# Cross-attention with image-prompt tokens: the store of a block's second query tile moves into the next round

## The reference

```python
q = _split_heads(hidden_states @ w_q, HEADS)
k = _split_heads(text @ w_k, HEADS)
v = _split_heads(text @ w_v, HEADS)
out_text = _merge_heads(_sdpa(q, k, v))
mask_ip = _ip_mask(bbox, B, S, hidden_states.dtype)
k_ip = _split_heads(ip_h @ w_k_ip, HEADS)
v_ip = _split_heads(ip_h @ w_v_ip, HEADS)
out_ip = _merge_heads(_sdpa(q, k_ip, v_ip, mask=mask_ip))
out = out_text + IP_SCALE * out_ip
out = out @ w_out + b_out
out = out + residual
```

## Time and profile before

| | |
|---|---|
| timed runs | 734.43, 734.0, 729.98 us (median 734.0) |
| profiled execution, device time | 729.49 us |
| its span, first to last instruction | 727.7 us |
| TensorE matmul busy | 688.1 us (95%) |
| VectorE busy | 540.1 us (74%) |
| ScalarE, POOL busy | 288.3 us (40%), 213.5 us (29%) |
| mean granted TensorE clock | 0.979 |

### The profile page before, as it was taken

One profiled execution on the slowest core, in us unless ns is written; L12 is line 12 of the kernel. 1 busy time (PEld: TensorE's weight loads), 2 busy tenths in 40 slices (PEclk: granted clock), 3 DMA queues, 4 the chain that ended last, 5 costly groups with the idle time before them and its releaser, 6 DMA issues.

```text
span 727.7 us, 18922 instructions
## 1 busy us (share of the span) xinstructions
PE 688.1 (95%) x6410; PEld 628.2 (86%) x6410; DVE 540.1 (74%) x1686; ACT 288.3 (40%) x626; POOL 213.5 (29%) x359
## 2 busy tenths in 40 slices
PE   4979778999999999999999999999999999999987
PEld 3567467989999998989999999999999989899876
DVE  5341539878787979797878788787879797978764
ACT  1031117153534435261617162535444261617061
POOL 7100004324150504142423324151505042423223
PEclk9879999999999999999999999999999999999979
DMA  9935954253434444433435263534344444434310
GB/s 266 323 98 137 267 147 121 66 155 92 136 90 134 102 127 103 140 89 102 130 89 156 68 163 82 147 96 127 98 127 103 133 96 125 104 92 114 90 49 37
DMA packets 79543, 89.52 MB, mean 123 GB/s; under 512 B 10680, under 2 KB 63416, under 8 KB 79492
## 3 DMA queue, kind: packets, MB, share of 16 engines
q1 hardware_dynamic: 79016, 88.45, 44.7%
q10 hardware_dynamic: 492, 0.61, 0.4%
HBM read 39.21 MB, written 10.62 MB: 68 GB/s over the span
## 4 chain that ended last, share of the span: by engine, by line
PE 75%; DMA 8%; DVE 7%; SPq 6%; issue 2%; ACT 1%; ACTq 0%; POOL 0%; DVEq 0%
PE psum L1019 32%; PE psum L1124 9%; PE psum L1076 7%; PE psum L1108 6%; PE psum L1103 5%; DMA q_stack<-aux_a 4%; SPq L457 3%; PE psum L1132 3%; PE psum L901 3%; PE psum L1133 2%; SPq L429 2%; DMA wo_raw<-in_L_xattn_w_v_ip 2%; PE psum L1147 2%; PE psum L980 2%; PE psum L1130 1%
## 5 line engine op out<-in xcount | busy, mean ns | idle before, releaser
L522 POOL TENSOR_TENSOR attn<-o_parts 128x128 f32<-128x128 f32 x160 | 73.8, 461 | 418.9 <-DVE o_parts L844 418.9
L803 DVE TENSOR_REDUCE neg_max<-psum 128x2 f32<-128x292 f32 x320 | 144.7, 452 | 64.0 <-PE psum L1076 63.4
L1019 PE MATMUL psum<-wo_both,at_hi 128*128 128x320 f32 x640 | 153.2, 313 | 0.0
L1019 PE MATMUL psum<-xt_hi,wq_hi 128*128 128x256 f32 x400 | 114.9, 287 | 1.4 <-DVE xt_lo L773 1.4
L1076 PE MATMUL psum<-k_stack,q_stack 104*128 104x154 f32 x640 | 112.6, 286 | 3.5 <-DVE neg_max L804 1.5
L1019 PE MATMUL psum<-xt_hi,wq_lo 128*128 128x256 f32 x400 | 112.1, 280 | 0.0
L1019 PE MATMUL psum<-xt_lo,wq_hi 128*128 128x256 f32 x400 | 112.0, 280 | 0.0
L831 DVE TENSOR_TENSOR p_lo<-psum,p_hi 128x512 f16<-128x512 f32 x160 | 107.9, 682 | 2.8 <-ACT psum L657 2.8
L1019 PEld LDWEIGHTS psum<-wo_both,at_hi 128*128 128x128 f32 x640 | 109.6, 188 | 0.0
L655 ACT ACTIVATE p_hi<-psum 128x512 f16<-128x512 f32 x160 | 95.3, 595 | 27.8 <-PE psum L1103 27.7
L1124 PE MATMUL psum<-v_tail,p_tail 128*128 128x264 f32 x320 | 102.0, 400 | 2.6 <-DVE p_lo L831 1.6
(11 more groups left out here) (93 smaller groups left out, 1260.3 us busy)
## 6 DMA issues: line engine op xcount, KB each, us to landing
q_stack<-q_hi SPq DMA_DIRECT2D x128, 96.0 KB
x_in<-in_x SPq DMA_DIRECT2D x16, 640.0 KB, 4.1
x_res<-in_x SPq DMA_DIRECT2D x16, 640.0 KB, 5.1
out<-out_sb SPq DMA_DIRECT2D x32, 320.0 KB
q_stack<-q_hi SPq DMA_DIRECT2D x128, 64.0 KB
q_stack<-q_lo SPq DMA_DIRECT2D x64, 96.0 KB
q_stack<-q_lo SPq DMA_DIRECT2D x64, 64.0 KB
q_stack<-aux_a SPq DMA_DIRECT2D x48, 64.0 KB, 2.4
```

What stands on the lines that cost most here:

```text
L522: nc.gpsimd.tensor_tensor(cols, o_parts[:, qt, 0:4, :], o_parts[:, qt, 4:8, :], ALU.add).then_inc(att_half, 1)
L803: nc.vector.tensor_reduce(dst[:, :, 0], src[:, :, 0:TEXT], AX_X, ALU.max, negate=True)
L1019: last = nc.tensor.matmul(ps, l(c), r(c), start=(i == 0), stop=(i == len(terms) - 1))
```

## The change

The store of a block's second query tile is no longer the last step of SyncE's round. A new step ("LAST") does it in the next round, behind the three DMAs of set A's maxima and ahead of XIN and XRES. The second tile of the last block is stored after all rounds. Round 1 has no LAST, since no block is complete yet; rounds 2 to 16 have one each. The number of stores stays 32.

```diff
 SP_STEPS = [
-    (BACK, "AUX", 0), (NEXT, "XIN"), (BACK, "XRES"), (BACK, "AUX", 1), (FRONT, "STK", 0), (FRONT, "STK", 1),
-    (BACK, "STORE", 0), (BACK, "STORE", 1),
+    (BACK, "AUX", 0), (BACK, "LAST"), (NEXT, "XIN"), (BACK, "XRES"), (BACK, "AUX", 1), (FRONT, "STK", 0), (FRONT, "STK", 1),
+    (BACK, "STORE"),
 ]
...
                     if kind == "STORE":
-                        qt = args[0]
-
-                        sp.wait_ge(out_done, t * 4 - 4 + 2 * qt + 2)
-                        sp.dma_start(out_rows[bass.ds(t * QB - QB + qt * P, P), :], out_sb[:, qt, :]).then_inc(stored, 16)
+
+                        sp.wait_ge(out_done, t * 4 - 4 + 2)
+                        sp.dma_start(out_rows[bass.ds(t * QB - QB, P), :], out_sb[:, 0, :]).then_inc(stored, 16)
+                    if kind == "LAST" and not (isinstance(t, int) and t == 1):
+
+                        sp.wait_ge(out_done, t * 4 - 4)
+                        sp.dma_start(out_rows[bass.ds(t * QB - QB - P, P), :], out_sb[:, 1, :]).then_inc(stored, 16)
                 if not it.back:
                     before_aux()
 
             iterations(sp, body)
+
+            sp.wait_ge(out_done, 4 * BLOCKS)
+            sp.dma_start(out_rows[BLOCKS * QB - P:BLOCKS * QB, :], out_sb[:, 1, :]).then_inc(stored, 16)
```

## The result

The change makes the kernel a little faster: 729.55 us median of 20 runs (726.0 to 732.42), against 734.09 us (729.98 to 735.77) for the kernel before. The ratio is 0.9943, with a 95% interval of 0.9925 to 0.9961, so 2.9 to 5.5 us less. The forecast was 729.4 us.

A forecast was written before the change was run, and what follows sets the result against it. TensorE bounds the kernel, held by set A's late DMAs. Idle 6.3 − (0.87 − 0.28) − (1.2 − 0.08) = 4.6 us, taken off the 734.0 us median, gives 729.4 us; range 724.5 to 734.4 us.

The forecast's parts named there:

- The term of 4.6 us: TensorE's idle time before the first transposed scores, waiting for set A: 4.6 of 6.3 us won, bounds 2.4 to 5.2.
- rival 3: More than one place gains: round 2's long issue loses 0.8 us, or runs fall quicker by themselves; 727 us, chance 0.10.
- the end is the same: End of the kernel: the last tile's store follows the same add as before, so no time is won or lost.
- XRES's wait: SyncE's wait before the residual's load, now for a store just issued: landing taken as 3 us, cost nothing.
- bounds of 2.3 and 5.1: Store's landing time: 2.3 us from the kernel's last store, 5.1 us from a load twice the size behind another.
- the limit of 5.9 us of landing: SyncE before set B: the store behind set A may take 5.9 us to land without delaying set B's issue.
- rival 1: Store lands late, so SyncE starts set B and STK 0 late: 754.6 us at 8.2 us of landing, chance 0.05.
- this overlap: DMA engines before set B: bytes of store, x and residual in by about 309.5, set B issued at 310.1; price nothing.
- Rival 2: TensorE's wait comes back at the new block's scores, where the DMAs' cover is 0.46 us: 734 us, chance 0.12.
- its counterargument: New block's scores: STK 0 starts when TensorE's earlier steps let it, and those move up as well.
- the quicker half: Whole runs: the timed runs fall into their quicker half by themselves as the code is laid out anew.

The follow-up runs named there:

- experiment 3: The change with the old wait for the last residual add put back ahead of set A in rounds 2 to 16, store still behind set A: 729.23 us, 0.9938.
- experiment 4: The change with the second tile's store issued by ScalarE's queue at the beginning of the next round instead of by SyncE: 729.23 us, 0.9935.
- experiment 5: The change with LAST behind XRES and the wait guarding out_sb's second half moved from SyncE to VectorE: 727.9 us, 0.9933.

## Why the prediction was right

*The cause.* That set A's late start, and in it SyncE's own time, holds TensorE, is shown from three sides: half of the delay put back gives 38.60 us rounds, one issue more than that 39.07, the wait without the issue nothing.

*The term of 4.6 us.* Measured 4.1 and 3.9 us between the profile before and the two of the change (from set A's copy in round 2 to the end), and 4.2 us by the ratio. The loop rounds gave what was read from their waits of 0.36 to 0.40 us: they are 0.35 to 0.46 us shorter. That the whole comes out so close is partly luck, since three things that the forecast lacked nearly cancel:

- Round 2 gave its whole 0.87 us instead of 0.28. The issue that had taken 2.70 us for three DMAs took 2.05 and was ahead of the reader; in the second profile it took 1.87. This is a part of what rival 3 named. It isn't sure to come: in experiments 3, 4 and 5 the wait there is 0.55, 0.23 and 0.22 us.
- Round 8 lost 0.44 us in the first profile; in the second, rounds 2 and 9 lost 0.9 and 0.5 us.
- Behind the first transposed scores of round 16 the changed kernel took 0.9 us longer than before in the first profile and 0.8 in the second. The forecast had put this at nothing: "the end is the same".

In rounds 8 and 16 of the first profile SyncE has a long issue of set B:

```profile
390.23 2.21 SPq L429 DMA_DIRECT2D q_stack<-aux_b  x2
698.79 2.12 SPq L429 DMA_DIRECT2D q_stack<-aux_b  x2
```

In the second profile these two took 1.23 us each, and other ones were long. The kernel before has one of 2.03 us in round 8 too, without a longer round. So they belong to the execution rather than to the place; they come, as far as the profiles show, where a piece of code is run for the first time. Why is open. They don't explain the end, where the second profile lost nearly as much without one. What differs there is the granted clock, the third number from the end of each row: first before, then the second profile of the change, then the first.

```profile
696.60:700.60 4.00, 3.37 (x24) 2.68 (x23) 2.47 (x6) 3.40 (x7) 0.00 (x0) 0.50 0.13 22
700.60:704.60 4.00, 3.71 (x43) 3.12 (x41) 3.58 (x11) 3.09 (x6) 1.82 (x4) 0.94 0.10 15
...
695.10:699.10 4.00, 3.37 (x25) 2.68 (x23) 2.47 (x6) 3.40 (x7) 0.00 (x0) 0.50 0.15 28
699.10:703.10 4.00, 3.63 (x38) 2.95 (x35) 2.83 (x9) 3.15 (x6) 1.52 (x4) 0.72 0.10 15
...
697.10:701.10 4.00, 3.45 (x40) 2.84 (x40) 3.40 (x10) 3.97 (x9) 0.46 (x1) 1.00 0.17 43
713.10:717.10 4.00, 3.21 (x22) 2.85 (x23) 1.81 (x5) 0.66 (x2) 1.03 (x4) 0.60 0.01 4
```

The first two pairs both lie 4 to 12 us behind the step, and before the change the clock is back earlier. In the first profile it is back earlier still, but falls again near the end, and TensorE waits 1.7 us for set B. In experiment 3 the part from set A's copy in round 16 to the end takes 38.6 us, against 39.2 before and 40.3 and 40.1 in the two profiles. So the end varies by more than it differs here, and the change isn't shown to be the cause.

*XRES's wait.* The store landed 2.6 us after its start (307.02 to 309.64); I had taken 3 from bounds of 2.3 and 5.1, and so had XRES 2 to 2.5 us behind the load of x, where it is 1.9. Its price of nothing held, by experiment 5. By the Trainium skill (DMA: Bandwidth & Descriptors, Anatomy of one DMA, the fixed and variable cost table, fitted to DMAs that GpSimd issues) such a store takes 2.8 us, an estimate; the trace is close to it.

*Where I was wrong though the number held:* the limit of 5.9 us of landing and the price of rival 1, 14 us for each us beyond. I had computed when SyncE is late. The limit that binds first is the DMA engines': set B's landing behind x_res. I had named this overlap, called its cover thin and priced it at nothing, without working out what happens beyond it. Even the reading for the change itself was too short: I had the last bytes in 0.6 us before set B is issued, but in round 6 the DMA engines still moved 338 GB/s from 312 to 313 and 166 GB/s in the us after, and set B was issued at 313.34. Its landing of 2.4 us held all the same. Stores that should have landed early enough to be free cost 36 us, and a stall of 3.4 us cost 6.1 with what the clock added. With four stores in the place of one, 1280 KB, the same way of reckoning gave 729.6 to 731 us, and it took 765.8.

*The rivals.* Rival 2 (the wait comes back at the new block's scores) is new in one round only, round 8 with 0.57 us, and not there in the second profile. In the loops its counterargument held: from the mask's DMA to the reader it is 4.13 us in round 6 (322.85 to 326.98), against 4.15 before, so STK 0 did move up with TensorE. Of rival 3 the gain in round 2 came, the quicker half did not: both kernels keep their spread of 6 us, which goes with the mean granted clock, and the median lies in its middle.

## What to carry to other kernels

- A queue that waits for the end of a round and then issues something nobody waits for delays what stands behind it by the issue and by the loop's end. Put that issue behind the urgent one; half of the delay was not the DMA but the loop's end that followed it.
- Before a transfer is moved, count the bytes on the DMA engines in front of the next urgent one, not only the issuing engine's time. Find the edge by doubling the moved bytes: here one more store was free, three cost 36 us.
- Compare profiles from an event behind the parts that the change doesn't touch. Here one pair of spans said 1.3 us slower, where the kernel is 4 us faster.

## What the runs showed of the hardware

- SyncE starts a DMA 0.03 us after the copy it waited for has ended (set A in the change, set B in both kernels). In loop rounds one issue takes 0.38 to 0.40 us for a 320 KB store and 0.6 us for the broadcast of 64 KB; a loop's end stood for about 0.25 us of the old delay.
- A store of 320 KB from SBUF to DRAM counts up its semaphore 2.6 us after its issue began (2.55 to 2.9 over the rounds), also with a load of 640 KB issued right behind it.
- With three more stores, TensorE's granted clock stayed at 1.00 through stalls of 1.66 and 2.38 us and fell to 0.50 with stalls of 2.23 and 3.37 us. It also fell in round 16 of the kernel before, in the 4 us ahead of the first transposed scores, in which TensorE was busy for 2.08 us and its last wait was 1.25 us.
